# A mixture-of-experts tower: gate and up sums of the first two routed experts taken ahead of their weight rows, with the products kept in PSUM

## What is computed

```python
logits = einsum('th,eh->te', x, gate_w); scores = sigmoid(logits)
# 2 of 4 groups, then 8 of 32 experts per token; weights normalised, times 2.5
g = einsum('th,eih->eti', x, expert_gate)      # all 32 experts, for all tokens
u = einsum('th,eih->eti', x, expert_up)
outs = einsum('eti,ehi->eth', silu(g) * u, expert_down)
final = (gathered * topk_w[:, :, None]).sum(1) # an unchosen expert has weight 0
return final + shared_mlp(x)                   # the shared one has no router weight
```

## Time and profile before

| | before |
|---|---|
| median of 3 executions | 378.09 us (378.01 to 379.32) |
| the profiled execution | 377.62 us, its span 375.8 us |
| TensorE matmul busy | 350.1 us (93%) |
| VectorE, ScalarE, GpSimd busy | 239.1, 186.6, 137.6 us |
| mean granted TensorE clock | 0.982 |
| chain that ended last | PE 70%, DVE 15%, ACT 6%, issue 4%, DMA 3% |

### The profile page before, as it was taken

One profiled execution on the slowest core, in us unless ns is written; L12 is line 12 of the kernel. 1 busy time (PEld: TensorE's weight loads), 2 busy tenths in 40 slices (PEclk: granted clock), 3 DMA queues, 4 the chain that ended last, 5 costly groups with the idle time before them and its releaser, 6 DMA issues.

```text
span 375.8 us, 9905 instructions
## 1 busy us (share of the span) xinstructions
PE 350.1 (93%) x3943; PEld 297.0 (79%) x3943; DVE 239.1 (64%) x513; ACT 186.6 (50%) x372; POOL 137.6 (37%) x144
## 2 busy tenths in 40 slices
PE   8999998999979799999999999999999999889674
PEld 6855665777659799999999999999997788666343
DVE  4556889787869355555555555555554673766686
ACT  5267952695464334444444444444445784224171
POOL 0036742450441166565656544443310013410012
PEclk9999999999998989999999999999999999999699
DMA  8920001000650424454454443544200000000001
GB/s 294 400 115 1 4 3 30 1 3 3 190 150 0 138 61 138 134 150 147 148 148 148 146 138 120 145 141 145 87 0 2 0 2 5 3 4 2 1 0 65
DMA packets 14865, 32.08 MB, mean 85 GB/s; under 512 B 2480, under 2 KB 4464, under 8 KB 14576
## 3 DMA queue, kind: packets, MB, share of 16 engines
q1 hardware_dynamic: 13328, 30.48, 25.2%
q10 hardware_dynamic: 1504, 1.13, 0.9%
HBM read 30.91 MB, written 0.69 MB: 84 GB/s over the span
## 4 chain that ended last, share of the span: by engine, by line
PE 70%; DVE 15%; ACT 6%; issue 4%; DMA 3%; ACTq 1%; POOL 1%; SPq 1%; DVEq 0%; POOLq 0%
PE psum L1119 70%; DVE xn L813 1%; DMA km<-in_experts 1%; DVE nt L807 1%; ACT region L770 1%; DVE nt L809 1%; DVE nt L810 1%; DMA wb<-weights 1%; DVE rc L877 1%; DVE km L1101 1%; ACTq L550 1%; ACT sq L583 1%; POOL xl L525 1%; DVE pk L818 1%; SPq L375 1%
## 5 line engine op out<-in xcount | busy, mean ns | idle before, releaser
L1119 PE MATMUL psum<-xh,split_all 128*128 128x296 f32 x544 | 124.0, 302 | 1.9 <-DVE rt L1015 1.9
L482 POOL TENSOR_TENSOR split_all<-km,split_all 128x768 fp32r<-128x768 f32 x34 | 63.7, 1878 | 86.9 <-ACT split_all L691 86.9
L1119 PEld LDWEIGHTS psum<-xh,split_all 128*128 128x128 f32 x544 | 92.9, 190 | 2.3 <-DVE rt L1015 2.2
L1119 PE MATMUL psum<-xl,split_all 128*128 128x296 f32 (+1 forms) x288 | 85.7, 302 | 0.7 <-POOL xl L525 0.7
L711 ACT ACTIVATE ah<-rt 128x296 fp32r<-128x296 f32 x68 | 30.7, 452 | 79.5 <-DVE rt L1015 73.1
L1119 PEld LDWEIGHTS psum<-xl,split_all 128*128 128x128 f32 (+1 forms) x288 | 53.8, 189 | 1.7 <-POOL xl L525 1.1
L1017 DVE TENSOR_TENSOR al<-rt,ah 128x296 fp32r<-128x296 f32 x64 | 29.9, 468 | 33.1 <-ACT ah L711 33.1
L1012 DVE TENSOR_TENSOR rb<-psum,wb 128x296 f32<-128x296 f32 x64 | 29.9, 467 | 32.2 <-ACT psum L709 28.4
L1119 PE MATMUL psum<-ah,split_all 128*128 128x296 f32 x272 | 48.8, 301 | 0.4 <-ACT ah L711 0.4
L1119 PEld LDWEIGHTS psum<-ah,split_all 128*128 128x128 f32 x272 | 41.1, 190 | 0.6 <-ACT ah L711 0.6
L1015 DVE TENSOR_TENSOR rt<-rb,psum 128x296 f32<-128x296 f32 x64 | 29.6, 463 | 6.1 <-DVE rb L1012 1.7
(11 more groups left out here) (184 smaller groups left out, 556.2 us busy)
## 6 DMA issues: line engine op xcount, KB each, us to landing
km<-in_experts SPq DMA_DIRECT2D x34, 384.0 KB, 4.0
wb<-weights SPq DMA_DIRECT2D x32, 296.0 KB, 3.7
w_sb<-in_w SPq DMA_DIRECT2D x2, 1024.0 KB, 8.3
region<-in_x SPq DMA_DIRECT2D x6, 296.0 KB, 4.8
region<-in_w_lin ACTq DMA_DIRECT2D x6, 128.0 KB, 5.3
qkv_sb<-in_qkv_w SPq DMA_DIRECT2D x1, 768.0 KB, 4.7
cst<-in_consts SPq DMA_DIRECT2D x1, 502.5 KB, 7.2
out<-x SPq DMA_DIRECT2D x2, 148.0 KB, 1.8
```

The lines of the kernel that those rows point to most:

```text
L482: nc.gpsimd.tensor_tensor(wl[i], ring[i], wh[i].bitcast(f32), ALU.subtract)\
L1119: return nc.tensor.matmul(out_, lhsT, rhs, start=start, stop=stop, skip_group_check=True)
```

## The change

`up_sums` is divided into `gate_sums` and `linear_sums`. TensorE's hand-written order over units 2 and 3 becomes: gate and up sums of half 5 (banks 6 and 7), gate and up sums of half 6 (banks 5 and 7), down sums of 4, down sums of 5, gate and up sums of half 7 (banks 4 and 6), down sums of 6, gate and up sums of half 8, down sums of 7. On ScalarE and VectorE the order for these four halves is written out: silu goes to SBUF (`sg`, the name `ra` in the profile) for halves 4 to 6, VectorE multiplies it with the up sums first and leaves the product in PSUM, and the product with the weight row comes second. For half 7 silu goes to bank 7, the weight row is multiplied first and the up sums second. The router's chain, its stores, SP's order, GpSimd's order and everything from half 8 on stay.

```diff
@@ -717,10 +717,29 @@
                         act_e.wait_ge(s_wtr, 1)
                         for q in range(2, 4):
                             store_weights(act_e, q)
-            for i in range(SHARED, NRING):
-                expert_unit(2 * i, 0, ps[6][:, 0:HALF])
-                high_part(i + AHEAD, (i + AHEAD) % NRING, (i + AHEAD) // NRING)
-                expert_unit(2 * i + 1, 1, ps[7][:, 0:HALF])
+            def silu(n, gate, bank):
+
+                act_e.wait_ge(s_g, n + 1)
+                nc.scalar.activation(gate, ps[bank][:, 0:HALF], ACT.Silu).then_inc(s_sg, 1)
+
+            def rounded(n):
+
+                act_e.wait_ge(s_act, n + 1)
+                nc.scalar.activation(ah[:, n % 2, :], act[:, n % 2, :], ACT.Copy).then_inc(s_ah, 1)
+
+            silu(4, sg[:, 0, :], 4)
+            silu(5, sg[:, 1, :], 6)
+            high_part(4, 0, 1)
+            act_e.wait_ge(s_mulc, 1)
+            silu(6, sg[:, 0, :], 5)
+            rounded(4)
+            rounded(5)
+            act_e.wait_ge(s_mulc, 3)
+            silu(7, ps[7][:, 0:HALF], 4)
+            act_e.wait_ge(s_down, 5)
+            rounded(6)
+            high_part(5, 1, 1)
+            rounded(7)
             with act_e.Fori(1, (UNITS - AHEAD) // NRING) as r:
                 for i in range(NRING):
                     u = r * NRING + i
@@ -1017,10 +1036,40 @@
                 nc.vector.tensor_tensor(al[:, j, :], act[:, j, :], ah[:, j, :].bitcast(f32), ALU.subtract)\
                     .then_inc(s_al, 1)
 
-            for u in range(SHARED, NRING):
-                dve.wait_ge(s_wb[u], 16)
-                for j in range(2):
-                    expert_unit(2 * u + j, j, ps[6 + j][:, 0:HALF], wb[:, u, half(j)])
+            def early_product(n, gate, up_bank, out_):
+
+                dve.wait_ge(s_sg, n + 1)
+                dve.wait_ge(s_u, n + 1)
+                nc.vector.tensor_tensor(out_, gate, ps[up_bank][:, 0:HALF], ALU.mult).then_inc(s_mulc, 1)
+
+            def low(n):
+
+                dve.wait_ge(s_ah, n + 1)
+                nc.vector.tensor_tensor(al[:, n % 2, :], act[:, n % 2, :], ah[:, n % 2, :].bitcast(f32), ALU.subtract)\
+                    .then_inc(s_al, 1)
+
+            early_product(4, sg[:, 0, :], 5, ps[4][:, 0:HALF])
+            early_product(5, sg[:, 1, :], 7, ps[6][:, 0:HALF])
+            dve.wait_ge(s_wb[2], 16)
+            dve.wait_ge(s_mulc, 2)
+            for j in range(2):
+                nc.vector.tensor_tensor(act[:, j, :], ps[4 + 2 * j][:, 0:HALF], wb[:, 2, half(j)], ALU.mult).then_inc(s_act, 1)
+            low(4)
+            low(5)
+            early_product(6, sg[:, 0, :], 7, ps[5][:, 0:HALF])
+            dve.wait_ge(s_wb[3], 16)
+            dve.wait_ge(s_mulc, 3)
+            dve.wait_ge(s_al, 1)
+            nc.vector.tensor_tensor(act[:, 0, :], ps[5][:, 0:HALF], wb[:, 3, half(0)], ALU.mult).then_inc(s_act, 1)
+            dve.wait_ge(s_sg, 8)
+            nc.vector.tensor_tensor(gu[:, 1, :], ps[7][:, 0:HALF], wb[:, 3, half(1)], ALU.mult).then_inc(s_mulc, 1)
+            dve.wait_ge(s_down, 5)
+            low(6)
+            dve.wait_ge(s_u, 8)
+            dve.wait_ge(s_mulc, 4)
+            dve.wait_ge(s_al, 2)
+            nc.vector.tensor_tensor(act[:, 1, :], gu[:, 1, :], ps[6][:, 0:HALF], ALU.mult).then_inc(s_act, 1)
+            low(7)
             with dve.Fori(1, UNITS // NRING) as r:
                 for i in range(NRING):
                     dve.wait_ge(s_wb[i], r * 16 + (16 if i >= SHARED else 0))
@@ -1472,6 +1521,22 @@
                 mm(out_, w_hi, x_lo, False, False)
                 return mm(out_, w_lo, x_hi, False, stop)
 
+            def gate_sums(u, i, hf, bank):
+
+                for c in range(C):
+                    cols = slice(c * INNER, (c + 1) * INNER)
+                    ins = three(ps[bank][:, 0:HALF], (wh[i][:, cols], wl[i][:, cols]),
+                                (xh[:, c, half(hf)], xl[:, c, half(hf)]), c == 0, c == C - 1)
+                ins.then_inc(s_g, 1)
+
+            def linear_sums(u, i, hf, bank):
+
+                for c in range(C):
+                    cols = slice(D + c * INNER, D + (c + 1) * INNER)
+                    ins = three(ps[bank][:, 0:HALF], (wh[i][:, cols], wl[i][:, cols]),
+                                (xh[:, c, half(hf)], xl[:, c, half(hf)]), c == 0, c == C - 1)
+                ins.then_inc(s_u, 1)
+
             def up_sums(u, i, hf, bank=4, waits=None):
 
                 n = 2 * u + hf if waits is None else waits
@@ -1479,18 +1544,10 @@
                     pe.wait_ge(s_wsl, u + 1)
                 if waits != 0:
                     pe.wait_ge(s_sg, n)
-                for c in range(C):
-                    cols = slice(c * INNER, (c + 1) * INNER)
-                    ins = three(ps[bank][:, 0:HALF], (wh[i][:, cols], wl[i][:, cols]),
-                                (xh[:, c, half(hf)], xl[:, c, half(hf)]), c == 0, c == C - 1)
-                ins.then_inc(s_g, 1)
+                gate_sums(u, i, hf, bank)
                 if waits != 0:
                     pe.wait_ge(s_act, n)
-                for c in range(C):
-                    cols = slice(D + c * INNER, D + (c + 1) * INNER)
-                    ins = three(ps[bank + 1][:, 0:HALF], (wh[i][:, cols], wl[i][:, cols]),
-                                (xh[:, c, half(hf)], xl[:, c, half(hf)]), c == 0, c == C - 1)
-                ins.then_inc(s_u, 1)
+                linear_sums(u, i, hf, bank + 1)
 
             def down_sums(u, i, hf, shared=False):
                 n = 2 * u + hf
@@ -1525,11 +1582,19 @@
             down_sums(1, 1, 0, shared=True)
             up_sums(2, 2, 0, 4, 3)
             down_sums(1, 1, 1, shared=True)
-            for u in (2, 3):
-                up_sums(u, u, 1)
-                down_sums(u, u, 0)
-                up_sums(u + 1, (u + 1) % NRING, 0)
-                down_sums(u, u, 1)
+            up_sums(2, 2, 1, 6, 4)
+            pe.wait_ge(s_wsl, 4)
+            pe.wait_ge(s_mulc, 1)
+            gate_sums(3, 3, 0, 5)
+            pe.wait_ge(s_mulc, 2)
+            linear_sums(3, 3, 0, 7)
+            down_sums(2, 2, 0)
+            down_sums(2, 2, 1)
+            gate_sums(3, 3, 1, 4)
+            linear_sums(3, 3, 1, 6)
+            down_sums(3, 3, 0)
+            up_sums(4, 0, 0)
+            down_sums(3, 3, 1)
             with pe.Fori(1, (UNITS - 1) // NRING) as r:
                 for i in range(NRING):
                     u, nxt = r * NRING + i, (i + 1) % NRING
```

## The result

| | before | changed |
|---|---|---|
| median | 378.05 us (376.57 to 380.15, 12 runs) | 376.13 us (373.57 to 378.55, 12 runs) |
| ratio changed to before | | 0.9936, 95% interval 0.9907 to 0.9965 |
| profiled execution, its span | 377.62, 375.8 us | 375.75, 374.0 us |
| mean granted clock in the profiled execution | 0.982 | 0.995 |

The change is faster by 0.64%, which is 2.4 us of 378.05, the interval reaching from 1.3 to 3.5 us. The two medians differ by 1.9 us. I had said 3.0 us and 375.1 us, with a range of 374.0 to 377.0.

The account below looks back on a forecast made before the run. The router and its DRAM round trip bound up to 130.3 us, TensorE alone behind it. Of 3.70 us lost, two short waits of 0.35 and 0.37 leave 2.98 won: 378.09 less 3.0 gives 375.1 us, range 374.0 to 377.0.

Parts of the forecast that it names:

- The bound and the 3.70 us: Router's DRAM round trip bounds up to 130.3 us, then TensorE; 12 groups take 13.50 against 9.80 us, 3.70 lost.
- Three groups into the bubble: Half 5's up sums and half 6's gate and up sums, 2.45 us, fill TensorE's 2.08 us idle without a wait.
- A wait for the new product in PSUM: Sign of being wrong: half 6's up sums, due at 129.86, would wait for half 5's product, expected by 129.75.
- The row's slack of half a microsecond: The weight row, landing at 129.2 us, is there half a microsecond before VectorE comes to it.
- The first short wait: TensorE ahead of half 4's down sums waits for the high part: 0.25 us plus 0.1 for the restart, 0.35.
- The second short wait: TensorE ahead of half 6's down sums, whose high part stands behind half 7's silu: 0.27 + 0.10 = 0.37 us.
- The sum: Half 9's gate sums start at 127.41 + 9.80 + 0.35 + 0.37 = 137.93 us, against 140.91, 2.98 us sooner.
- The clock: Costed at nothing: TensorE idles only 0.25 and 0.27 us where it idled 1.93, so no fall behind 131 us.
- the first and second rivals: Clock falls behind 131 us: once, costing 1.65 us, 376.8 us (0.11); or a long fall, costing 3.0 us (0.05).
- The third rival: A wait holds half 6's up sums, so two groups fill the bubble; gain 1.6 to 2.5 us, chance 0.09.
- The fourth: Rival: the short waits vanish, gain up to 3.70 us, 374.4 us; chance 0.05.
- From the stretch to the total: The gain between half 5's and half 9's gate sums is carried whole to the end, TensorE being the bound.

Follow-up runs that it names:

- The filled kernel: The kernel before with 14 idle-filling matmuls on TensorE ahead of half 5's up sums, real work in the old order: 377.30 us, ratio 0.9990 to before.
- half 6 first: The changed kernel with half 6's high part ahead of half 7's silu and its low part ahead of half 7's weighted silu: 375.52 us, ratio 0.9910 to before.
- before again: The kernel before, unedited, run for another profile: 378.67 us, ratio 1.0005 to before.
- before with the early fill: The kernel before with six idle-filling matmuls on TensorE between the router's matmuls of the two halves: 378.33 us, ratio 1.0003 to before.
- second pair: The kernel before and the changed kernel, both unedited, each run for another profile: 378.67 us and 376.09 us.
- the rounding alone: The changed kernel with ScalarE rounding the weights of units 4 and 5 after the high parts of halves 5 and 7: 375.86 us, ratio 0.9929 to before.
- both edits: The changed kernel with the weights of units 4 and 5 rounded later and half 6 finished before half 7's silu: 375.50 us, ratio 0.9921 to before.
- both with the early fill: The changed kernel with later rounding, half 6 before half 7's silu, and six idle-filling matmuls among the router's: 373.97 us, ratio 0.9897 to before.

## Why the prediction was right, point by point

**The bound and the 3.70 us** were read rightly. The filled kernel divides them: 2.1 us of waiting, 1.3 to 1.4 of low clock, and the rest in small waits that I had put down to the clock. What I had not seen is that the low clock behind the bubble is not always there to be won. It was in all three profiles of before (the third with the early fill). But of 86 executions of before for which the mean granted clock is known, ten have 0.995, as much as the changed kernel's first profile, which has a single fall of 3.4 us before its last microsecond. All twelve profiles have a fall near 350 us, so in those ten there is no room for one behind the bubble.

**Three groups into the bubble.** The up sums of half 5 and the gate sums of half 6 ran without a wait. The up sums of half 6 waited some 0.1 us for the product in PSUM, which I had put at zero with a slack of 0.16: VectorE ended it at 129.62, and TensorE's matmuls at 129.55 are 0.24 apart instead of 0.14. The product took 0.47 us as taken. "A wait for the new product in PSUM" was one of my signs of being wrong; it came, but at a tenth of a microsecond.

**The row's slack of half a microsecond** held: no wait for it, and a row 2.15 us later cost VectorE 1.5. I had the rows issued 0.33 us apart, which is the length of one issue; they start 0.38 to 0.48 apart. Nothing rests on it, as the second row landed at 129.90 and was wanted at 132.5.

**The first short wait** is the term of the sum that was mis-sized. I had put 0.25 + 0.10 = 0.35 us for the high part of half 4. It measured 130.46 + 0.14 = 130.60 to 132.09, 1.49 us for a group of 0.82, so 0.67. The high part came sooner than I had it, 0.15 us late; what I had called ready "before its turn", the low part of half 4, was 0.33 us late and made TensorE restart a second time. I moved the rounding of unit 4's weights ahead and had written that GpSimd's subtraction would start sooner as if that cost nothing. It now ran beside VectorE's low part, and the run with it later showed that this is the whole of the 0.3 us. The Trainium skill (SBUF — State Buffer, SBUF: two separate sides) states that the two engines share a pair of SBUF ports as an exclusive lock for a whole instruction, and counts among the cases a VectorE operation with two SBUF inputs against a GpSimd operation that reads SBUF. By that rule a low part that begins beside the subtraction ends after it; the trace agrees (0.84 to 1.53 us instead of 0.47), and VectorE's products with one operand in PSUM kept their 0.47 us beside it. I had not weighed it.

**The second short wait**: 134.54 to 135.73 for a group of 0.82, 0.37 lost, as put. The order of ScalarE made it, as the run with half 6 first shows.

**The sum**: 9.80 + 0.10 + 0.67 + 0.37 is 10.94, measured 10.91; forecast 10.52. The gain at this place is 2.59 instead of 2.98 us.

**The clock** did not fall: the first and second rivals did not come to pass. The clock stayed at 1.00 behind two waits of 0.15 to 0.3 us, and in the other runs behind single ones of 1.48 and 1.69; behind 1.93 (before), 2.14 (before again) and 1.92 us (before with the early fill) at the same place it fell each time. The Trainium skill (TensorE: Matmul & The Clock Gate, A second HAM failure mode: psum-queue depth-cycling) has frequent short idles between groups of matmuls make the clock swing; no run here shows that. The mean clock rose by 0.013 where I had forecast 0.004, and that was luck of the execution: beside the fall behind the bubble, the one near 114 us was missing and the one near 350 us half as long. In the second pair the mean clock was 0.982 in both kernels.

**The third rival** was right in its mechanism, that a wait holds the early work, but only for 0.1 us. **The fourth** was off: the short waits did not vanish by themselves; with two edits all but 0.33 us did.

**From the stretch to the total**, I carried the gain whole to the end. The rest of the experts took 148.6 us in both profiles, so no steady wait swallowed it. The total's 2.4 us with its interval of 1.3 to 3.5 holds both 2.6 and 3.0. The two medians' 1.9 us are within what the other stages vary by.

## What to carry to other kernels

Where one engine waits for a round trip, count first the work that needs nothing of it, and move enough for the whole wait: one group of three, with VectorE's order left as for three, won nothing beyond the clock, and three of three won 2.6 of 3.7 us, of which 1.3 to 1.4 was the clock that no longer falls. Then look at what the moved orders bring together on the other engines: here a GpSimd subtraction that came beside a VectorE operation with two SBUF inputs, and a silu that stood ahead of a conversion TensorE wanted sooner. When the effect is of the size of a run's spread, compare the stretch between two fixed instructions in several profiles, and let the total only confirm it.

## What the runs showed of the hardware that I had not expected

The same program's executions differ by 5 us (375.48 to 380.47 for before in 28 runs, 376.25 to 381.44 in 31 others), and the profiles say where. TensorE's waits without a releaser in the last attention add up to between 0.5 and 2.8 us in the twelve profiles and move about. The rest of the experts, a loop in which TensorE stops only once, for 0.4 us, takes 148.6 us in eight of the twelve profiles and 147.6 in four, 0.817 or 0.811 us a group, at a granted clock of 1.00 in both; before shows both values. Why, I did not find.

The clock falls between 107 and 116 us in seven of the twelve profiles, for 3.4 us and once for 6.8, and in the others not. Near 350 us it falls in all twelve, at TensorE's wait of 3.3 us, for 3.4 or 6.8 us. Three profiles have one more fall, at 363 to 365 us, and what follows the scaling of the last bias takes 7.1 us there instead of 6.0. They are the three of kernels in which the weights are rounded later (the rounding alone, both edits, and both with the early fill). Whether the edit has a part in it three profiles can't say; if it has, it gives back 1 us of what it wins.

In the second profile of the changed kernel the long fall near 114 us put TensorE 0.9 us later against the router's sigmoid. I had written of the early fill in before that such a lateness only shortens the wait for the row. It does not: the weight row, too, landed 0.9 us later there (16.8 instead of 15.9 us after the sigmoid), so the row came 1.8 us behind the start of half 5's gate sums in both of its profiles.
